# Finishing a node block one step later on VectorE in the two relational layers of a graph network kernel

## The reference

```
def _rgcn_conv(x, src, dst, edge_type, W_r, W_root, b):
    seg = dst * r + edge_type
    msg = x[src]
    agg = segment_sum(msg, seg, n * r).reshape(n, r, d)
    cnt = segment_sum(ones, seg, n * r).reshape(n, r, 1)
    mean = agg / maximum(cnt, 1.0)
    out = einsum('nrd,rdk->nk', mean, W_r)
    return out + x @ W_root + b
...
for l in range(2):
    conv = relu(_rgcn_conv(h, src, dst, edge_type, W[l], root[l], bias[l]))
    res = relu(h @ res_W[l] + res_b[l])
    h = conv + res
return x + h
```

## Time and profile before

| what | before |
|---|---|
| median of 3 runs | 13214.41 us (13211.8 to 13218.76) |
| the profiled execution | 13230.24 us |
| its span | 13228.4 us |
| busy: POOL / DVE / PE / ACT | 8081.2 / 5540.5 / 5033.2 / 2257.5 us |
| layer 1 | about 3.7 to 8.55 ms of the span |
| layer 2 | about 8.56 to 13.2 ms of the span |

### The profile page before, as it was taken

How to read it: one execution, slowest core, us unless ns; L and a number is a source line. 1 busy time by engine, 2 the same in 40 slices (tenths; PEclk the granted TensorE clock), 3 DMA queues, 4 the chain that set the end, 5 groups by cost and what they waited for, 6 DMA issues and landing times.

```text
span 13228.4 us, 141611 instructions
## 1 busy us (share of the span) xinstructions
PE 5033.2 (38%) x39273; PEld 3527.8 (27%) x39273; DVE 5540.5 (42%) x20233; ACT 2257.5 (17%) x5671; POOL 8081.2 (61%) x8294
## 2 busy tenths in 40 slices
PE   3556666666633333333333333322222222222222
PEld 3434444444412222222122222211111111111112
DVE  6754444444445556555556656511111111111111
ACT  4733333333311111111111111100000000000000
POOL 7355555554556666666666666566666666666666
PEclk5677777777766666566656556655555555555555
DMA  2122222222333333333333333311111111111111
GB/s 74 39 70 92 91 89 89 89 92 95 98 123 115 119 124 117 117 124 122 116 119 124 117 117 124 122 24 24 24 24 24 24 24 24 24 24 24 24 24 33
DMA packets 485431, 1012.62 MB, mean 77 GB/s; under 512 B 191444, under 2 KB 237540, under 8 KB 484548
## 3 DMA queue, kind: packets, MB, share of 16 engines
q1 hardware_dynamic: 227204, 742.28, 15.1%
q0 software_dynamic: 257920, 266.40, 10.6%
HBM read 558.25 MB, written 453.13 MB: 76 GB/s over the span
## 4 chain that ended last, share of the span: by engine, by line
another core or an unknown queue 45%; DVE 29%; PE 12%; issue 11%; ACT 2%; DVEq 1%; DMA 1%; SPq 0%; ACTq 0%; POOL 0%; POOLq 0%
DVE w_raw L1504 8%; DVE onehot L1496 5%; DVE w_parts L1496 5%; PE y_ps L1137 5%; DVE same_more L1504 3%; PE block_ps L1224 3%; DVE ystage L1459 2%; PE y_ps L1216 1%; PE sums_ps L1189 1%; ACT scr L936 1%; DVE w_room L1510 1%; DMA y_table<-ystage 1%; DVE step_val L1509 1%; PE signs_ps L1216 0%
## 5 line engine op out<-in xcount | busy, mean ns | idle before, releaser
L798 POOL DMA_INDIRECT rows<-y_table,idx_st x3234 | 3054.0, 944 | 1847.8 <-issue 1094.0
L798 POOL DMA_INDIRECT w_parts<-y_table,idx_st x3212 | 3032.8, 944 | 1664.8 <-issue 937.5
L798 POOL DMA_INDIRECT rows<-h_table,idx_st x1452 | 1662.2, 1145 | 1330.8 <-PE sums_ps L1189 683.9
L1565 DVE TENSOR_SCALAR rr<-rr 128x64 f32<-128x64 f32 x198 | 40.8, 206 | 4476.4 <-remote 4333.0
L1137 PE MATMUL y_ps<-scr,hT 128*128 128x512 bf16 (+1 forms) x2673 | 836.1, 471 | 2566.4 <-ACT hT L912 1814.7
L902 ACT ACTIVATE idx_st<-edges 128x11 int32 (+1 forms) x720 | 141.6, 211 | 8300.8 <-remote 6757.0
L1327 PE MATMUL sums_ps<-onehot,rows 128*64 128x64 f32 x6468 | 812.2, 286 | 1538.6 <-issue 1479.9
L1327 PE MATMUL sums_ps<-w_parts 128*64 128x64 f32 x6424 | 803.2, 285 | 1461.9 <-issue 1443.0
L926 ACT ACTIVATE ystage<-y_ps 128x512 f32<-128x512 f32 (+1 forms) x1782 | 995.4, 567 | 1401.2 <-PE y_ps L1137 879.1
L1327 PEld LDWEIGHTS sums_ps<-onehot,rows 128*64 128x64 f32 x6468 | 684.7, 196 | 1687.3 <-issue 1626.6
L1327 PEld LDWEIGHTS sums_ps<-w_parts 128*64 128x64 f32 x6424 | 674.8, 194 | 1611.5 <-issue 1563.3
(11 more groups left out here) (226 smaller groups left out, 7204.6 us busy)
## 6 DMA issues: line engine op xcount, KB each, us to landing
y_table<-ystage SPq DMA_DIRECT2D x396, 768.0 KB
edges<-key_row SPq DMA_DIRECT2D x198, 832.0 KB
y_table<-ystage SPq DMA_DIRECT2D x198, 608.0 KB
w_raw<-key_row SPq DMA_DIRECT2D x99, 832.0 KB
rows<-y_table,idx_st POOLq DMA_INDIRECT x3234
w_parts<-y_table,idx_st POOLq DMA_INDIRECT x3212
rows<-h_table,idx_st POOLq DMA_INDIRECT x1452
rr<-y_table SPq DMA_DIRECT2D x198, 64.0 KB
```

The source lines that it names most:

```text
L798: pool.indirect_dma_start(out=rows_of(l, u)[:, j, k, 0:D], out_offset=None, in_=table, in_offset=bass.IndirectOffsetOnAxis(ap=idx_of(l, u, ...
```

## The change

In layers 1 and 2, step s of DVE no longer finishes block s behind the one-hots of its second group, but block s-1. The first step of each layer finishes nothing, and block S-1 is finished behind the loop, ahead of the tail block. The first two steps are written out ahead of the loop, which now has 48 rounds. No instruction of DVE is added or dropped over a layer. PE, ACT, POOL and SP have the same instructions in the same order.

```
-                    with dve.Fori(0, S // 2) as i:
-                        s_half[0] = i
+                    def late_step(i, u, first=False):
+                        s = i * 2 + u
+                        s_par[0], s_half[0] = u, i
+                        take_step(l, s, u)
+                        for j in range(J):
+                            q = s * J + j
+                            if l == 1:
+                                weigh(q, j, s)
+                            make_onehot(l, q, j)
+                            if j == 1 and not first:
+                                s_par[0], s_half[0] = 1 - u, i if u else i - 1
+                                finish_block(l, s - 1)
+                                s_par[0] = u
+
+                    for u in range(2):
+                        late_step(0, u, first=u == 0)
+                    with dve.Fori(0, S // 2 - 1) as i:
                         step.enter(i, {1: 2 * (7 + 2 * J), 2: 2 * 4}[l])
                         for u in range(2):
-                            s = i * 2 + u
-                            s_par[0] = u
-                            take_step(l, s, u)
-                            for j in range(J):
-                                q = s * J + j
-                                if l == 1:
-                                    weigh(q, j, s)
-                                make_onehot(l, q, j)
-                                if j == 1:
-                                    finish_block(l, s)
-                        step.leave(S // 2)
+                            late_step(i + 1, u)
+                        step.leave(S // 2 - 1)
                     s_half[0] = None
-                    for s in TAILS:
+                    for s in (S - 1, *TAILS):
                         finish_block(l, s)
```

## The result

| what | before | after |
|---|---|---|
| median, measured side by side | 13215.85 us (13211.8 to 13218.76) | 13890.23 us (13881.95 to 13903.02) |
| ratio after/before | | 1.0512 (95%: 1.0499 to 1.0526) |
| span of the profiled execution | 13228.4 us | 13880.1 us |

A forecast was written before the change was run, and what follows sets the result against it. POOL's gathers set the step, held back by PE, which is slow while POOL gathers. 13230.2 profiled + 725 (layer 1) - 30 (layer 2) = 13925, less 15.8 for the median: 13,910 us; range 12,900 to 14,800.

The forecast's parts named there:

- A round over the keys closes in layer 1 and sets the step: Layer 1: key loads behind transform bound the step at 56.7 us, +7.4 us a step, +725 us in all.
- Which keys: Layer 1: the keys of groups 0 and 1 set the round; group 2's link takes no more.
- the 20.9 us: Layer 1: time from the start of transform(s) to the key loads of groups 0 and 1.
- One slow and one fast group: DVE in layer 1: of groups 0 and 1, one takes 19.3 us and the other 9.8 us.
- The way to the load: Layer 1, SP: group 2's keys are loaded 11.1 us after transform starts.
- the landing: Layer 1: arrival of the first key load after issue, taken as 4.0 us, between nearly nothing and 7.8 us.
- Layer 2: One-hots ready earlier for PE change a step by -0.3 us, -30 us over 98 steps.
- rival B: Faster: in layer 2 POOL skips every other pause, saving 343 us (12,870) to 627 us (12,590); chance 0.20.
- the bound of +5.5 us: Layer 2's upper bound a step: a longer POOL run would cost 53 us a step against 47.6.
- A: Layer 1's loop stays hidden, both groups fast, 47.2 us under 49.3; no change, 13,190 to 13,240 us; chance 0.08.
- C: Layer 1, both groups slow: 66.2 us a step, +1656 us, about 14,870; chance 0.18, most of the way included.
- D: POOL's gathers lengthen under VectorE work, 0.1 us each, 3.3 us a step, +320 us; chance 0.01.

The follow-up runs named there:

- e4: Changed kernel with all key loads issued ahead of the saves, those of groups 0 and 1 a step earlier; 13159.29 us, ratio 0.9956.
- e3: Changed kernel with group 2's key load issued right behind those of groups 0 and 1, ahead of the saves; 13288.75 us, ratio 1.0056.
- e5: Changed kernel with only the keys of groups 0 and 1 loaded a step earlier, on the second kind of chip; 11206.37 us, ratio 1.0314.
- e12: Repeat: changed kernel with only the keys of groups 0 and 1 loaded a step earlier, second kind of chip; 11208.97 us, ratio 1.0315.
- e10: Changed kernel without an edit, against the kernel before on the second kind of chip; 11217.12 us, ratio 1.0324.
- e1: Kernel before with the new order in layer 2 alone; 13184.48 us, ratio 0.9975.
- e8: Kernel before with one gather instead of 11 in each group of layers 1 and 2, sums wrong; 6671.28 us.

## Why the prediction was right, and where it was not

- *A round over the keys closes in layer 1 and sets the step: right.* Forecast 56.7 us a step, measured 56.5; e4 takes the keys out of the round and the loss is gone.
- *Which keys: wrong.* The prediction took its sum over the keys of groups 0 and 1, and said of group 2's that their link "takes no more than the round above has". In its figures the two ways were a tie. From the start of transform until VectorE can begin group 0 they take 20.9 + 4.0 = 24.9 us over the keys of groups 0 and 1, and 11.1 + 4.0 + 9.8 = 24.9 us over group 2's keys and group 2 itself. Behind that both go on through groups 0 and 1. The step that failed is the 20.9 us. It was read from a step of before in which the last third of transform stood in a slow stretch; its last chunk waited for ACT:

```profile
6028.44 0.66 PE L1137 MATMUL y_ps<-scr,hT 128*128 128x192 bf16 x3 [7.55 <-ACT ystage L926]
```

  In the changed kernel the whole transform runs within 11 us, and these loads come 11.7 us after its start. That makes 11.7 + 6.2 = 17.9 us by the one way and 8.1 + 6.2 + 9.0 = 23.3 by the other, so the round over group 2's keys binds, by about 5 us. e3 shows 6.2 us a step from moving that one load, and e5 and e12 against e10 show nothing from moving the others.
- *The terms.* Along the way that binds, the prediction's own figures give 11.1 + 4.0 + 9.8 + 19.3 + 9.8 + 1.9 + 0.8 = 56.7 us. Measured are 8.1, 6.2, 9.0, 20.9, 9.1 and 2.8, together 56.1. One slow and one fast group was right. The way to the load came out 3.0 us too long and the landing 2.2 us too short, and that these cancel is luck; so is it that the sum over the wrong keys was as long as the one over the right ones. The landing was the middle of bounds from 0 to 7.8 us; 6.2 us pass from the issue to the first weighing. By the fit of the Trainium skill ("DMA: Bandwidth & Descriptors", the anatomy of one DMA) the landing would be 4.0 us and the round 53.9, an estimate. The traces don't agree, with 6.2 and 6.7 us (e10), though those contain other traffic and the semaphore.
- *Layer 2: right in size.* Forecast -0.3 us a step, -30 us; -32 us in the trace, -35 us in e1. The mechanism of rival B did begin, in that POOL passes one group more between pauses, but the pause grew from 6.65 to 8.4 us, as the 10.38 us of the earlier trace rows had suggested. The prediction's price for a longer run was a misreading, though. Between its two rows, 8559.41 and 8665.62, the trace has not 66 gathers but 77:

```profile
L798 POOL DMA_INDIRECT rows<-y_table,idx_st x44: 940/944/947, 8559.4 to 8654.3; - x44
L798 POOL DMA_INDIRECT w_parts<-y_table,idx_st x33: 940/944/955, 8600.6 to 8640.6; - x33
```

  106.2 us over 77 gathers are 45.5 us for 33, not 53, so the longer run was cheaper than 47.6 and the bound of +5.5 us a step has nothing behind it. That -0.3 came out, between bounds of which one was wrong, is luck in part.
- *Rivals.* A has what e4 shows, a step of 49.3 us, and only with the keys moved. C, with both groups slow, did not happen: group 1 takes 9.1 us. D: L798 takes 947 ns in the mean of layer 1 (5000 to 8000 us) against 944:

```profile
L798 POOL DMA_INDIRECT rows<-y_table,idx_st x889 | 841.8, 947 | 690.1 <-ACT idx_st L902 435.8 <-issue 254.3
```

  3 ns over 33 gathers are 0.1 us a step.

## What to carry to other kernels

When a step's work is put off behind other work on its engine, draw each round that goes through the moved instruction and back to it, with every buffer whose refill stands behind the result on an in-order queue, and add all that the engine does on the way. The longest of them bounds the step, even if the engine is 40% busy over the span and had 7 us to spare. Where two rounds come out alike, work out both: a term read from the kernel before can shrink with the change, as the 20.9 us did. Then move the refill ahead of the saves before moving the work: here that turned 5.1% of loss into 0.4% of gain on the first chip, and 3.2% of loss into nothing gained or lost on the other kind.

## What the runs showed of the hardware

The same program takes 13,220 us on the chip of e1 to e4, 13,216 us in the measurement of the result, and 10,866 us on two other chips. Layers 1 and 2 hold 1421 of these 2350 us: 98 steps of 49.3 and 47.6 us on the one, of 41.2 and 41.2 on the others. What the traces show to be different are the stretches in which POOL gathers without a pause. On the slower chip PE starts its matmuls there one at a time, here in layer 2 of the changed kernel:

```profile
11039.92 0.26 PE L1327 MATMUL sums_ps<-w_parts 128*64 128x64 f32 x1 [1.84 <-issue]
11042.02 0.27 PE L1327 MATMUL sums_ps<-w_parts 128*64 128x64 f32 x1 [1.83 <-issue]
11044.12 0.27 PE L1327 MATMUL sums_ps<-w_parts 128*64 128x64 f32 x1 [1.83 <-issue]
11046.92 0.26 PE L1327 MATMUL sums_ps<-w_parts 128*64 128x64 f32 x1 [2.54 <-issue]
```

On the other, 22 follow each other in 2.6 us as soon as the rows have come (e10, layer 2):

```profile
8513.70 2.61 PE L1327 MATMUL sums_ps<-onehot,rows 128*64 128x64 f32 x22 [10.42 <-DMA rows<-y_table,idx_st]
8527.52 2.58 PE L1327 MATMUL sums_ps<-onehot,rows 128*64 128x64 f32 x22 [10.16 <-DMA rows<-y_table,idx_st]
```

On the slower chip the starts lie multiples of 0.7 us apart. VectorE shows the same in such a stretch: in layer 1 of the changed kernel weighings start at 6080.93, 6082.32, 6085.12 and 6087.22. On the other chips the step is 33 gathers without a pause, 41.2 us in both layers, and the cost of the change falls from 5.1% to 3.2%: the round is 11 us shorter without the slow group 0, and POOL's step 8 us shorter. What causes the stretches stays open. e8 was to say whether fewer gathers end them, but it ran on a chip that shows none.
